# Four unread products before the input projection of each state-space layer, and a decay table written earlier

## The reference, cut to what matters

```python
h = jnp.transpose(x, (0, 2, 1))
for i in range(NL):                        # NL = 4
    z = _layernorm_channels(h, ln_w[i], ln_b[i])
    z = _s4d_layer(z, log_dt[i], A_re_log[i], A_im[i], C_re[i], C_im[i], D_skip[i], W_out[i], b_out[i])
    h = z + h
...
def _s4d_layer(z, ...):
    dtA = A * dt[:, None]
    C = (C_re + 1j * C_im) * (jnp.expm1(dtA) / A)
    K = 2.0 * jnp.einsum('hn,hnl->hl', C, jnp.exp(dtA[:, :, None] * l)).real
    y = irfft(rfft(z) * rfft(K))           # a causal convolution of length 2048
    y = jax.nn.gelu(y + z * D_skip[:, None])
    out = jnp.einsum('oh,bhl->bol', W, y) + bvec[None, :, None]
    return out[:, :Hh] * jax.nn.sigmoid(out[:, Hh:])
```

## Time and profile before

| | us |
|---|---|
| median of three runs | 1269.58 |
| the three runs | 1269.18, 1269.58, 1277.02 |
| profiled execution, its own time | 1262.45 |
| span of the profiled execution, first to last instruction | 1260.7 |
| TensorE busy / VectorE / ScalarE / GpSimd | 1013.1 / 756.0 / 535.7 / 410.6 |
| mean granted TensorE clock | 0.892 |

### The profile page before, as it was taken

One profiled execution on the slowest core, in us unless ns is written; L12 is line 12 of the kernel. 1 busy time (PEld: TensorE's weight loads), 2 busy tenths in 40 slices (PEclk: granted clock), 3 DMA queues, 4 the chain that ended last, 5 costly groups with the idle time before them and its releaser, 6 DMA issues.

```text
span 1260.7 us, 20058 instructions
## 1 busy us (share of the span) xinstructions
PE 1013.1 (80%) x7980; PEld 678.4 (54%) x7980; DVE 756.0 (60%) x1322; ACT 535.7 (42%) x1226; POOL 410.6 (33%) x458
## 2 busy tenths in 40 slices
PE   6796698777445289999999967859979988979888
PEld 3464556564323167878787742324456643546643
DVE  2516558574757534646464578969946646956654
ACT  4473646636223311222212060016768635668742
POOL 1216411514206500000000044447944343964420
PEclk9995886978676589999999978979989999979999
DMA  3340170807114264554723030000012210011101
GB/s 101 67 70 8 36 138 23 153 9 144 30 34 202 70 140 101 93 107 60 138 45 57 16 146 0 1 0 1 1 46 58 64 67 26 1 35 40 48 18 33
DMA packets 60431, 76.50 MB, mean 61 GB/s; under 512 B 37452, under 2 KB 41944, under 8 KB 58584
## 3 DMA queue, kind: packets, MB, share of 16 engines
q1 hardware_dynamic: 60348, 75.36, 26.4%
HBM read 52.87 MB, written 1.51 MB: 43 GB/s over the span
## 4 chain that ended last, share of the span: by engine, by line
PE 52%; DVE 19%; POOL 13%; ACT 6%; issue 6%; DMA 3%; SPq 1%; POOLq 0%; DVEq 0%
PE psum L1239 7%; PE psum L1241 7%; PE psum L1240 7%; POOL rest L1491 3%; POOL rest L1481 3%; POOL rest L1487 2%; PE psum L713 2%; PE psum L1734 2%; PE psum L605 2%; PE psum L1727 2%; ACT rest L1425 2%; PE psum L1780 2%; DMA rest<-share_d 2%; POOL rest L1517 2%; DVE main L1581 1%
## 5 line engine op out<-in xcount | busy, mean ns | idle before, releaser
L406 POOL TENSOR_TENSOR kept<-kept 128x8 f32<-128x8 f32 x8 | 1.6, 203 | 392.0 <-DVE kept L383 392.0
L1425 ACT ACTIVATE rest<-psum,main 128x128 f32<-128x128 f32 x256 | 113.4, 480 | 11.4 <-POOL main L1502 8.9
L1086 ACT ACTIVATE x_high<-main 128x512 fp32r<-128x512 f32 x48 | 30.3, 633 | 199.0 <-DVE main L1160 199.0
L1239 PE MATMUL psum<-x_high,w_low 128*128 128x512 f32 x192 | 76.7, 400 | 20.0 <-DVE x_low L1165 20.0
L1517 POOL TENSOR_TENSOR rest<-rest,main 128x512 f32<-128x512 f32 x64 | 65.4, 1044 | 45.5 <-DVE main L1587 45.5
L1239 PE MATMUL psum<-hid_high,w_low 128*128 128x512 f32 x192 | 75.6, 394 | 0.7 <-DVE main L1184 0.7
L1240 PE MATMUL psum<-x_low,w_high 128*128 128x512 f32 x192 | 76.1, 397 | 0.0
L1241 PE MATMUL psum<-x_high,w_high 128*128 128x512 f32 x192 | 76.1, 396 | 0.0
L1240 PE MATMUL psum<-hid_low,w_high 128*128 128x512 f32 x192 | 74.8, 389 | 0.0
L1241 PE MATMUL psum<-hid_high,w_high 128*128 128x512 f32 x192 | 74.7, 389 | 0.0
L1160 DVE TENSOR_TENSOR main<-kept,rest 128x512 f32<-128x512 f32 x48 | 33.0, 690 | 67.9 <-PE psum L1241 43.8
(11 more groups left out here) (322 smaller groups left out, 2784.4 us busy)
## 6 DMA issues: line engine op xcount, KB each, us to landing
rest<-share_d SPq DMA_DIRECT2D x4, 3072.0 KB, 21.4
rest<-share_d SPq DMA_DIRECT2D x4, 2304.0 KB, 20.2
main<-main SPq DMA_DIRECT2D x32, 256.0 KB, 6.4
main<-k_pad SPq DMA_DIRECT2D x16, 512.0 KB, 7.9
rest<-main SPq DMA_DIRECT2D x32, 256.0 KB, 3.7
main<-w_dram SPq DMA_DIRECT2D x2, 3072.0 KB, 14.0
main<-rest SPq DMA_DIRECT2D x32, 128.0 KB, 2.3
rest<-tables_dram SPq DMA_DIRECT2D x2, 2048.0 KB, 9.5
```

The costliest lines, as they stand in the source:

```text
L1239: T.matmul(dst, w_small, x_large, start=first, stop=False)
L1425: last = A.activation(probs[:, p, 4 * r + m, :], bank[2 * p + r][:, m * P:(m + 1) * P], ACT.Exp, scale=row_scale[:, c, r, m:m + 1], bias=r ...
```

## The change

Two edits. After the last product of the norms N = 1, 2, 3 TensorE makes four products `centre` x `hT[:, 0:512]` into PSUM bank 0, with no wait before them and no semaphore behind them. Nobody reads them; the in-products that follow overwrite the bank. And GpSimd writes the decay table of layer L + 1 within layer L, after the coefficients of L + 2 and ahead of `weighted`, in place of at the head of layer L + 1. Only layer 0 still writes its own.

```diff
@@ s4_pe_layer
                 s4_pe_z(pe, N, 2)
                 s4_pe_var(pe, N, 3)
                 s4_pe_z(pe, N, 3)
+                for _ in range(4):
+                    nc.tensor.matmul(bank[0][:, :], centre, hT[:, 0:512], start=True, stop=True)
             else:
                 s4_pe_glu(pe, L, 3)
@@ s4_pool_layer
-            s4_pool_decay(pool, L)
+            if L == 0:
+                s4_pool_decay(pool, 0)
             if more:
                 s4_pool_phases(pool, chain, L + 1)
                 if L + 2 < S4_LAYERS:
                     s4_pool_coefficients(pool, chain, L + 2)
+                s4_pool_decay(pool, L + 1)
                 s4_pool_weighted(pool, L + 1)
                 s4_pool_norm(pool, L + 1)
```

## The result

| | before | after |
|---|---|---|
| median of 15 runs | 1269.63 | 1261.89 |
| lowest and highest | 1266.26 to 1280.03 | 1250.63 to 1270.12 |
| profiled execution | 1262.45 | 1254.60 |
| span | 1260.7 | 1252.8 |

The ratio after to before is 0.9942, with a 95% interval of 0.9914 to 0.9970: 7.4 us faster (3.8 to 10.9), within 1% and inside the predicted range, but little more than half of the 13.0 us of the forecast.

The account below looks back on a forecast made before the run. The prediction took the serial passage between norm and in-products (VectorE's z copies, TensorE's in-products, VectorE's last transpose) as the bound. 4.9 + 9.9 - 0.9 - 0.9 = 13.0 us gave 1256.6 us, range 1251.5 to 1265.5.

Parts of the forecast that it names:

- (a): Seam after the norm: with the decay moved, VectorE's second z copy ends at 191.6 in place of 193.25.
- (b): Seam: four unread products end at 191.73, in-products start 1.63 us earlier; three seams, 4.9 us.
- (c): In-products of layers 1 to 3 at full clock take 3.85 us each, gaining 9.9 us in all.
- the rival of half clock in them: In-products stay at half clock; only the earlier start remains, 4.9 us, 1264.7 us; chance 1 in 10.
- (d): Faster in-products meet "issue" pauses: 0.3 us a seam, bounds 0 and 1.5, minus 0.9 us in all.
- limited by issue, not clock: In-products pause as L738 did in layer 0, taking 6.7 us; gain 6.1 us, 1263.5 us; chance 0.09.
- two others: In-products staying at half clock (1264.7 us, 1 in 10); VectorE's second copy not getting faster (1264 us, 0.07).
- (e): Layer 1's output products L738 start at half clock after longer idleness: 0.4 to 1.5 us lost, minus 0.9.
- The median carried over: Whole kernel: the median's 7.1 us above the profiled execution was kept, 1269.6 - 13.0 = 1256.6 us.

Follow-up runs that it names:

- decay alone: Against the kernel before: the decay table moved as in the change, the four unread products left out; ratio 0.9954 to the kernel before.
- shifted list: Against the changed kernel: 32 tiny unread products added at the very start of TensorE's list, 128 instructions more; one run, 1266.56 us.
- eight products: Against the changed kernel: eight unread products a seam in place of four; ratio 0.9968 to the kernel before.

## Why the prediction was right in direction and too large

- *The seam bounds, and the decay holds the copy* ((a), (b)): right. In-products start 1.54 us earlier after the last L675 group, 1.63 were forecast; 0.58 us for the second copy, 0.46 forecast. The unread products end within 0.3 us of the copy, as a tie should. Without the decay's move they are worth nothing (ratio 0.9998).
- *The granted clock is held* ((c)): right for the start of the in-products, and the rival of half clock in them fell: 1.00 in layers 2 and 3 and 0.91 in layer 1 of the changed kernel. To the end it held less often: over the seven kernels with four products and the moved decay, 21 seams, it fell within the in-products in 12. The pace at 1.00 is 14.8 to 15.6 ns, forecast 15.0. The pauses are another matter. By the floor of about 25 ns between starts of matmuls in the Trainium skill ("TensorE: Matmul & The Clock Gate", section "Wait — 56ns, not 53.3ns?"), whose example is at the full clock alone, 256 in-products would take at least 6.4 us, an estimate from that page; measured are 3.78 us, so it does not bind these.
- *Stalls given back* ((d)) **is the step that failed.** I took 0.3 us a seam, out of 0 to 1.5, from the in-products of layer 1 at half clock; the pauses in those of the changed kernel at full clock were 1.03, 1.20 and 1.29 us, and up to 1.99 in other kernels with the same seams. Over the same 21 seams the mean seam is 10.2 us (9.6 to 11.5) and the in-products take 5.7 us: 3.8 of work at the full clock, 1.5 of pause and 0.4 for the parts at half clock. (c) and (d) together are then 21.4 - 17.2 = 4.2 us, where 9.0 were forecast; of what is missing the pauses have 3 x (1.5 - 0.3) = 3.6 us and the clock within the in-products 1.2. The row that told of it stood in my own list, L738 at full clock with 1.07 and 1.54 us; I should have taken that one, since it was the nearest in instructions per microsecond.
- *The rival "limited by issue, not clock"* (0.09) had this mechanism. It gave 6.7 us for the in-products and a gain of 6.1 us; measured are 5.7 and 7.4, nearer to it than to the forecast's 3.85 + 0.3 and 13.0. It is wrong as worded, since the clock still gave 7.05 - 5.7 = 1.3 us a seam, but it deserved more than 0.09. That the time lies within the range is owed to the range's having been drawn out to this rival and two others; the forecast's own range, 1252 to 1261, was missed by 0.9 us.
- *Clock lost later* ((e)): the size was 2.0 us in layer 1, 0.9 forecast, and the place was another. L738 of layer 1 kept 1.00, after only 0.71 us of idleness, not 3 to 5. It starts 24.13 us after the end of the in-products, as before, and the exponents, which were to profit from the clock, ran at 0.50 (195.30 to 202.40), so TensorE was done later, not sooner. The clock fell behind L738, within L613 (226.92), which it began at 1.00 after 2.04 us of idleness. A kernel with in-products near half clock (decay alone, 56.9 us) shows the long stretch too, and two with in-products at full clock don't (shifted list 54.6, eight products 55.0). So a cost of the change is not shown here; the 54.3 of the one profiled execution before is the shortest of twelve.
- *The median carried over*: the sum was made from the profile and set against runs 7 us above it. The layer 0 copy explains a difference of 7.8 us between executions, and how many of each kind a median holds moves it by some microseconds. It is not the only such difference: the first norm's last L675 group starts at 89.0 us in one trace and at 96.6 in another (101.4 with the shifted list), and what makes that difference is open. That the runs of before are a mixture of the two kinds is inferred from their spread; only profiled executions show the copy.

Mean seams and the stretch behind layer 1 (56.2 us in the mean of the seven kernels, 54.3 before) give 3 x (13.2 - 10.2) - 1.9 = 7 us, near the 7.4 of the ratio. Part of that agreement is luck, since the 54.3 is one execution's and low.

## What to carry to other kernels

Unread products are worth something only where they fill the whole gap up to the moment at which the real ones can start; here that took another edit, which removed what held the last input back. That edit alone gave 5.6 us in the seams; the four products took it to 8.8 in the mean of the seven kernels, and the time of the runs doesn't show the difference. Before pricing a stretch at full clock, look how long the densest run at full clock lasts in the trace, its "issue" pauses included, and not only its pace. And look for copies of VectorE that end half a microsecond after some GpSimd instruction, whatever their size: moving or delaying the GpSimd work was worth more here (5.6 us in the seams, 3.4 in layer 0) than the clock (3.3).

## What the runs showed of the hardware

- TensorE pauses of 1.0 to 2.0 us in runs of 512 instructions at full clock, always at the same place counted in 256s of its list; adding 128 instructions far ahead moves it. Every one ends 1.2 to 1.6 us after a 16 KB packet of the instruction queue. In in-products at 0.50 from start to end there is none of over 0.3 us; one of 0.57 us stands in output products at 0.50 (shifted list, layer 3). With 7 us of slow products ahead, two of three seams had none.
- A 64x512 copy from SBUF to SBUF on VectorE takes 0.6 us alone, 2.3 behind one GpSimd instruction, and in some executions 8.65 us behind four, with the same list of instructions on both engines.
- After 1.5 us without work TensorE's clock was still 1.00 in six seams of six, and in five of them it fell within the in-products, once although they ran without a pause; after 3.2 us it was still 1.00 in one seam of three and 0.50 in two.
